# Four hand-set orders instead of one, and other PSUM banks and another order of the expert pairs for the last two batches

## The reference

```
x = x + L0_attn(layernorm(x))   # 16 heads of 8, softmax over 256 keys, relative positions clipped at 20
x = x + L0_ffn(layernorm(x))    # per token: attention of its 16 heads among each other, then 8 experts, softmax gate
x = x + L1_attn(layernorm(x))   # 8 heads of 16, second-order Taylor expansion of exp, linear attention
x = x + L1_ffn(layernorm(x))    # router, top 2 of 8 experts, and one shared expert
# an expert of L1_ffn: silu((x @ w1 + b1) * (x @ w3 + b3)) @ w2 + b2, hidden width 176
```

## Time and profile before

| what | value |
|---|---|
| median of 3 runs | 770.97 us (770.21 to 772.57) |
| the profiled execution's own time | 772.51 us |
| its span (first to last instruction) | 770.7 us |
| PE busy | 659.4 us (86%) |
| DVE busy | 554.9 us (72%) |
| ACT busy | 387.9 us (50%) |
| mean granted clock of PE | 0.955 |

### The profile page before, as it was taken

The page is one execution under the profiler, slowest core; times in us unless marked ns, Lnnn a source line. Parts: engine busy times, 40 slices in busy tenths (PEclk is TensorE's granted clock), DMA queues, the critical chain, the costliest instruction groups (busy, mean ns, idle before and its releaser), DMA issues. The chain is left out here.

```text
span 770.7 us, 16746 instructions
## 1 busy us (share of the span) xinstructions
PE 659.4 (86%) x6432; PEld 520.3 (68%) x6432; DVE 554.9 (72%) x1337; ACT 387.9 (50%) x907; POOL 146.0 (19%) x178
## 2 busy tenths in 40 slices
PE   2688566987999999999999999999998997787886
PEld 1567445765787788778777787678776874565655
DVE  2322578569768986899679977898679867876263
ACT  3365235446556754674556555656565544225240
POOL 2413201330233023300520051104220101011000
PEclk9999787999899999999999999999999999799798
DMA  5502000200110002000200011001100010000000
GB/s 126 217 1 22 15 1 1 26 12 2 14 16 9 1 15 22 9 1 2 27 17 1 2 23 21 1 2 21 16 1 2 8 16 1 0 8 1 0 8 7
DMA packets 75908, 13.43 MB, mean 17 GB/s; under 512 B 69803, under 2 KB 74933, under 8 KB 75701
## 3 DMA queue, kind: packets, MB, share of 16 engines
q1 hardware_dynamic: 73202, 10.78, 7.8%
q0 software_dynamic: 384, 1.05, 0.5%
q10 hardware_dynamic: 2244, 0.55, 0.3%
HBM read 8.95 MB, written 3.16 MB: 16 GB/s over the span
## 5 line engine op out<-in xcount | busy, mean ns | idle before, releaser
L475 ACT ACTIVATE pm<-bank,nmx 128x256 f32<-128x256 f32 x256 | 100.6, 476 | 129.5 <-DVE nmx L760 129.5
L760 DVE TENSOR_REDUCE nmx<-bank 128x2 f32<-128x512 f32 x128 | 82.2, 684 | 48.9 <-PE bank L1083 48.8
L1094 PE MATMUL bank<-w,pm 128*128 128x128 f32 x512 | 83.3, 288 | 22.4 <-ACT pT L483 15.5
L483 ACT ACTIVATE pT<-bank 128x512 f32<-128x512 f32 x128 | 77.0, 602 | 43.7 <-PE bank L1094 42.5
L1073 PE MATMUL bank<-kT,qbd 64*64 64x256 f32 x1024 | 90.1, 415 | 9.4 <-POOL qr L585 9.3
L1112 PE MATMUL bank<-tv,pT 128*128 128x128 f32 (+1 forms) x512 | 81.0, 281 | 7.5 <-ACT pT L483 7.5
L1094 PEld LDWEIGHTS bank<-w,pm 128*128 128x128 f32 x512 | 60.9, 147 | 37.8 <-ACT pm L475 20.8
L970 DVE SCALAR_TENSOR_TENSOR hu<-bank,w,ha 128x256 f32<-128x256 f32 x104 | 49.9, 481 | 48.8 <-ACT ha L540 48.5
L1112 PEld LDWEIGHTS bank<-tv,pT 128*128 128x128 f32 x512 | 68.9, 193 | 16.8 <-issue 8.2
L540 ACT ACTIVATE ha<-bank,w 128x256 f32<-128x256 f32 x104 | 49.8, 479 | 48.9 <-PE bank L1272 48.9
L1271 PE MATMUL bank<-xfT,w 128*128 128x256 f32 x208 | 66.4, 401 | 7.5 <-DVE hu L970 7.4
(11 more groups left out here) (202 smaller groups left out, 1305.8 us busy)
## 6 DMA issues: line engine op xcount, KB each, us to landing
w<-wpack_dram SPq DMA_DIRECT2D x1, 3944.0 KB, 12.2
xin<-x_in_dram SPq DMA_DIRECT2D x8, 128.0 KB, 2.1
d_qdh<-qdh SPq DMA_DIRECT2D x8, 128.0 KB, 2.1
d_rv<-rvs SPq DMA_DIRECT2D x64, 16.0 KB, 2.2
out_dram<-xo POOLq DMA_DIRECT2D x8, 128.0 KB, 2.6
qc<-d_qdh SPq DMA_DIRECT2D x15, 64.0 KB, 3.8
tv<-d_ev SPq DMA_DIRECT2D x1, 736.0 KB, 4.5
w<-wpack_dram SPq DMA_DIRECT2D x1, 513.0 KB, 4.5
```

Of the source, the lines that this page charges most:

```text
L475: a = act.activation(pm[:, s % 2, c, j], b_s[c][:, j * S:(j + 1) * S], exp, bias=nmx[:, i:i + 1])
L483: act.activation(view(pT, (c * RTC + 2 * s) * C * P, [[1, 2 * C * P]]), b_t[:], copy).then_inc(pT_ready[0], 1)
L760: v.tensor_reduce(nmx[:, i:i + 2], b_s[c][:].rearrange("p (j k) -> p j k", j=2), AX_X, ALU.max, negate=True).then_inc(max_ready[0], 1)
L1094: a = nc.tensor.transpose(b_t[:, (j * 2 + kc) * P:(j * 2 + kc + 1) * P], chunk(pm[:, s % 2, c, j], kc), ident)
```

## The change

1. **Places by engine.** TURNS becomes one list for each engine, from ENGINE_AT, which has 141 places for each of PE, ACT, DVE and POOL. MOVED shifts the places of batches 0, 6 and 7 (all engines alike). Pieces, batches and instructions stay the same; only the order on each engine's queue differs.
2. **Chunks in another order, for all batches.** IN_TURN makes chunk 3k and 3k+1 the main parts of experts 2k and 2k+1, and chunk 3k+2 their remainder. Joins 0 to 3 are now the expert pairs and join 4 the shared expert. Join n < 4 waits only for the hid_ready that covers its three chunks; in batches 6 and 7 the order places the joins between or right behind the chunks.
3. **Banks of L1_ffn in batches 6 and 7**: chunks in banks 0 and 3, turn_rw in bank 2, joins in banks 1 and 2 in turn.
4. **Batch 7 only**: experts alternate between banks 6 and 4; Taylor scores rotate over banks 6, 4 and 5.

```diff
+IN_TURN = [x for k in range(NP) for x in (2 * k, 2 * k + 1, NX + k)] + [NE]
...
-TURNS = [(t, piece) for _, _, _, t, piece in sorted([(t * STEP[k] + at, at, k, t, piece) for at, k, piece in PIECES for t in range(B)])]
+def in_turn(at):
+    placed = [(t * PERIOD + at[k] + (MOVED[t][k] if t in MOVED else 0), k, t) for k in range(len(ALL)) for t in range(B)]
+    return [(t, ALL[k]) for _, k, t in sorted(placed)]
+TURNS = {engine: in_turn(at) for engine, at in ENGINE_AT.items()}
...
+        def late_bank(t, name, n):
+            if t < B - 2:
+                return bank[3]
+            return {"route": bank[3], "chunk": bank[3 * (n % 2)], "turn_rw": bank[2], "join": bank[1 + n % 2]}[name]
+        def expert_bank(t, n):
+            return b_rv if t == B - 1 and n % 2 else b_a
+        def taylor_bank(t, h):
+            if t < B - 1:
+                return (b_b, b_a)[h % 2]
+            return (b_a, b_rv, b_o)[h % 3]
...
 # PE, experts
+                    elif t < B - 1:
+                        pe.wait_ge(*raised(acc_e, t, 2 * C * n))
+                    elif n == 1:
+                        pe.wait_ge(*raised(rv_kept, B, 0))
                     else:
-                        pe.wait_ge(*raised(acc_e, t, 2 * C * n))
+                        pe.wait_ge(*raised(acc_e, t, 2 * C * (n - 1)))
...
 # PE, taylor
-                    if n == 2:
-                        pe.wait_ge(*raised(o3t_ready, t, 1))
-                    pe.wait_ge(*raised(sq_ready, t, 2 * n))
+                    if t < B - 1:
+                        if n == 2:
+                            pe.wait_ge(*raised(o3t_ready, t, 1))
+                        pe.wait_ge(*raised(sq_ready, t, 2 * n))
+                    elif n == 0:
+                        pe.wait_ge(*raised(acc_e, t, 2 * NE))
+                        pe.wait_ge(*raised(x1_ready, t, 1))
+                    else:
+                        pe.wait_ge(*raised(sq_ready, t, 2 * n - 1))
...
 # PE, join
-                    if n == 0:
+                    late_free(t, "join", n)
+                    if n == NP:
+                        pe.wait_ge(*raised(rwT_ready, t, 1))
                         pe.wait_ge(*raised(hid_ready, t, HPAIRS))
+                    else:
+                        pe.wait_ge(*raised(hid_ready, t, (3 * n + 2) // 2 + 1))
...
+            def late_free(t, name, n):
+                before = late_before(t, name, n)
+                if before is None:
+                    return
+                was, k = before
+                if was == "route":
+                    pe.wait_ge(*raised(r_steps, t, 2))
+                elif was == "chunk":
+                    pe.wait_ge(*raised(u_ready, t, k + 1))
+                elif was == "turn_rw":
+                    pe.wait_ge(*raised(rwT_ready, t, 1))
+                else:
+                    pe.wait_ge(*raised(eo_acc, t, 2 * C * (k + 1)))
```

More of the change, by code:

```diff
@@ L323, in build, with late_before, turns @@
         block = ctx.enter_context(nc.Block())
[L325 to L335, removed]
+        def late_bank(t, name, n):
+            if t < B - 2:
+                return bank[3]
+            return {"route": bank[3], "chunk": bank[3 * (n % 2)], "turn_rw": bank[2], "join": bank[1 + n % 2]}[name]
+        def late_before(t, name, n):
+            used = [p for p in LATE if p[0] in ("route", "turn_rw", "join") or p[0] == "chunk" and p[1] < NCH]
+            same = [p for p in used[:used.index((name, n))] if late_bank(t, *p) is late_bank(t, name, n)]
+            return same[-1] if same else None
+        def expert_bank(t, n):
[4 more added lines that the diff above has]
+            return (b_a, b_rv, b_o)[h % 3]
+        def turns(engine, piece):
+            for t, (name, n) in TURNS[engine]:
                 piece(t, name, n)
@@ L549, in rest @@
                 elif name == "turn_rw":
-                    evict(t, rwT_ps, 1, rwT_ready, late_bank(t, NCH)[0:NX, 0:S], rwT[:], (eo_ps, t, 0))
+                    evict(t, rwT_ps, 1, rwT_ready, late_bank(t, "turn_rw", 0)[0:NX, 0:S], rwT[:], (eo_ps, t, 0))
             fill_ends()
             act.wait_ge(ones_set[0], 1)
-            turns(piece)
+            turns("ACT", piece)
         @block.gpsimd
@@ L639, in _ @@
             pool.wait_ge(ones_set[0], 1)
-            turns(piece)
+            turns("POOL", piece)
         @block.vector
@@ L1224, in rest @@
                             rows = half * P // 2
-                            a = mm((b_b, b_a)[half][:, kc * S:(kc + 1) * S], chunk(k3[rows:rows + P // 2], kc), q3h[rows:rows + P // 2, n],
+                            a = mm(taylor_bank(t, 2 * n + half)[:, kc * S:(kc + 1) * S], chunk(k3[rows:rows + P // 2], kc), q3h[rows:rows + P // 2, n],
                                    start=True, stop=True, tile_position=(rows, 0))
@@ L1266, in rest @@
                     if n < NCH:
[L1267 to L1272 removed]
+                        late_free(t, "chunk", n)
@@ L1273, in rest @@
+                        bk, q = late_bank(t, "chunk", n), IN_TURN[n]
+                        mm(bk[:, 0:S], wc("W1", q * P, q * P + P), xfT[:], start=True, stop=True)
+                        mm(bk[:, S:2 * S], wc("W3", q * P, q * P + P), xfT[:], start=True, stop=True).then_inc(ab_ps[0], 1)
                 elif name == "turn_rw":
                     pe.wait_ge(*raised(rw_ready, t, 1))
-                    pe.wait_ge(*raised(u_ready, t, NCH + 1 - late_banks(t)))
+                    late_free(t, "turn_rw", 0)
@@ L1276, in rest @@
                     for c in range(C):
-                        a = nc.tensor.transpose(late_bank(t, NCH)[0:NX, c * P:(c + 1) * P], rw[:, c], ident)
+                        a = nc.tensor.transpose(late_bank(t, "turn_rw", 0)[0:NX, c * P:(c + 1) * P], rw[:, c], ident)
                     a.then_inc(rwT_ps[0], 1)
                 elif name == "join":
-                    dst = late_bank(t, n + 1)
-                    if n == 0:
+                    dst = late_bank(t, "join", n)
+                    late_free(t, "join", n)
@@ L1305, in _ @@
             pe.wait_ge(w_in0[0], 16)
-            turns(piece)
+            turns("PE", piece)
 def kernel(**inputs):
```

71 lines of the change are left out of this document (33 added, 38 removed), and 39 rows, old and new, of tables (ENGINE_AT, MOVED).

## The result

| | before | after |
|---|---|---|
| median, run side by side | 771.77 us (770.21 to 775.05, 4 runs) | 739.84 us (737.42 to 742.6, 4 runs) |
| the profiled execution's own time | 772.51 us | 742.6 us |
| its span | 770.7 us | 740.8 us |
| mean granted clock of PE | 0.955 | 0.964 |

What follows compares the result with a forecast made beforehand. PE was taken to bind in the middle and batch 7's chain in the tail. Terms 0.9 + 1.6 + 1.6 + 2.2 + 7.5 + 6.0 = 19.8 us, off 770.97, gave 751.2 us; range 742 to 762.

Steps and rivals of the forecast that it cites:

- from turn3 to route: Batch 7's Taylor scores to route: 7.5 us gained through extra banks and new order, bounds 3 and 9.
- The sign on batch 7's x1: A check on the mechanism: DVE finishes batch 7's x1 within 3 us of 633, against 635.7 before.
- L1_ffn of batch 7: Last stretch: joins start earlier and the 2.56 us wait goes; 6.0 us gained, bounds 3 and 7.
- the head: Batch 0's start: work moves ahead of the relative values' DMA wait and transposes move away; 0.9 us gained.
- The middle: Full batches: the wait for the routing weights' copy is hidden, 0.4 us each, 1.6 us over four.
- The bound of idle time: In the middle only PE's idle time can be won: at most 4.1 us a batch, some 20 in five.
- the wait for the routing weights: PE's wait for their copy in full batches, 0.4 us each, hidden by pieces between turn_rw and join 0.
- the middle gains as well: Rival: half of the 4.1 us idle goes in each of five batches, 10 us, giving 741 to 745; chance 0.12.
- Up to norm3: Batch 7 from x1 to norm3: 1.2 us from DVE's earlier mix sum plus 2.2 in the experts.
- The experts: Batch 7's experts: bank waits and products between them go, norm3 comes earlier; 2.2 us gained, bounds 0 and 3.
- The clock falls: Rival: PE's half-clock stretches in the tail stay or move, costing 4.8 or 5 us, giving 756 to 761; chance 0.13.
- The order holds up the tail: Rival: late PE joins stop DVE, half of the tail's 7.5 and 6.0 us goes, 758 to 762; chance 0.10.

Runs made afterwards that it cites:

- e3: The changed kernel with the old order on all engines from batch 0's project_out to batch 7's; 748.05 us, ratio to before 0.972.
- e7: The changed kernel with the old order on all engines, except ACT's new order up to batch 0's project_out; 762.93 us, ratio to before 0.988.
- e4: The changed kernel with the old order on all engines behind batch 7's project_out, new banks and waits kept; 748.31 us, ratio to before 0.972.
- e6: e4 with batch 7's old banks and their old waits for experts and Taylor scores; 752.53 us, ratio to before 0.975.
- e5: e4 with every join of a pair in batches 5, 6 and 7 also waiting for the last hid_ready; 753.96 us, ratio to before 0.974.
- e12: The changed kernel with only PE and ACT in the old order from batch 0's project_out to batch 7's; 755.02 us, ratio to before 0.982.
- e11: The changed kernel with the old order, except PE's and ACT's new order up to batch 0's project_out; 753.96 us, ratio to before 0.980.
- e1: The changed kernel with all four engines in the old order up to batch 0's project_out; 744.88 us, ratio to before 0.968.
- e2: The changed kernel with only ACT in the old order up to batch 0's project_out; 745.21 us, ratio to before 0.967.
- e8: The changed kernel with batch 7's chunks rotating over four banks (0, 3, 6, 7); 739.71 us, ratio to before 0.958.
- e9: The changed kernel with batch 7's chunks over four banks and its tanh in two buffers; 738.52 us, ratio to before 0.959.
- e10: The changed kernel with two tanh buffers in batch 7, chunks still in banks 0 and 3; 739.32 us, ratio to before 0.961.

## Why the prediction was wrong

**The direction and the tail were right.** 7.5 us from turn3 to route were forecast and 7.5 measured, with the signs that it named: 28 us, clock 1.00, the shared expert in 2.5 us (708.39 to 710.86). The sign on batch 7's x1 failed: it was to be within 3 us of 633 and is at 624.4. For L1_ffn of batch 7 6.0 were forecast, 5.7 came. The 2.56 us wait is gone, and from the last main chunk on the joins follow one another.

**The step that failed is the head.** The sum took 0.9 us for it, 5.8 came (by one profile each, and the head varies by some 2 us, see the last section). The 0.9 was worked out from the one wait at 77.4 us and the transposes at 84.34, the end of the head. For what lies before, the text looked at the page's clock and at no timeline. There batch 0 is alone with its scores, ACT and PE hand each other pm and pT, and PE waits for pT 6.8 us in seven places. The diff has a MOVED row for batch 0 alone, which said that this stretch would change.

**The middle was too small.** Of 5.5 us, 2.0 were in the sum. The bound of idle time was right (20 us), and so was the guess that the full batches give little: 0.5 us each by e3, 0.3 between before and after, where 0.4 were forecast for the wait for the routing weights. That wait is indeed gone from PE's list in the full batches (1.3 us in three before), but waits for ACT's squares came in (3.8 us in five). But "middle" was read from a full batch and applied to all. The first gap (73.4 us before, 70.9 after) and the last (76.5 and 75.5) aren't as full as the others (PE works 53.7 of 73.5 us in the first, 70.9 of 76.5 in the last), and by e3 they are worth 2.7 and 1.9 of the 7.4. The rival "the middle gains as well" (10 us, 741 to 745) named the direction, but with 2 us in each full batch, which did not come.

**Up to norm3** 3.4 us were forecast (1.2 and 2.2), 5.5 came. The experts gave 2.3 (8.6 to 6.3), so that term held. The stretch ahead of them gave 3.2 instead of 1.2. The sum had no clock in it for this stretch, and the mean clock there rose from 0.84 to 0.93. Why it rose is not shown: the joins of batch 5 no longer wait for their last chunk, which the text left out, but e7 has that too and keeps the 0.84.

**The causes were credited wrongly inside a right number.** In the tail the text ascribed the clock and the waits to order and banks together, and I expected e4, without the order, to lose most of it. It lost 4.8 of 18.6 us. The joins' early start and the banks carry more than the order.

**The rivals.** "The clock falls" did not come where it was priced, from turn3 on: the clock is at 1.00 from 650 us on. Between batch 7's x1 and there it still fell, to 0.50 at 648 us. The Trainium skill (TensorE: Matmul & The Clock Gate, "A second HAM failure mode: psum-queue depth-cycling") ties a swinging clock to cycling through banks with short idle times between groups. The runs agree in that: with the old banks (e6) the waits of 0.46 and 1.19 us and the half clock come back together. That more banks need not help was my own inference in the prediction; the section says nothing of the number of banks. It did not hold here: with a third bank the 1.19 us wait fell to 0.62, and the clock from turn3 to route is 0.95 in e4 instead of 0.85 in e6. Banks alone don't secure it either: e5 has them and is at 0.86. "The order holds up the tail" did not happen with these four lists, and e12 shows that it was no idle fear: in the middle, two new lists with two old ones cost 14.6 us against four new ones, and 7.2 against four old ones.

**The sum by the runs.** From before to e7, banks and expert pairs: 1.2%, 9 us. From e7 to e11, PE's and ACT's order in the head: 0.9%, 7 us. From e11 to the change, all other order: 1.9%, 15 us.

## What to carry to other kernels

Cut a pipelined kernel at the same marks in every batch and read every stretch between, the first batch's above all: a full batch tells nothing of those where the pipeline fills and empties, and this order by hand gave most there. Lists for engines are one object: change all that hand work to each other or none, since half a change gained 0 in the head and lost 7 us in the middle. Where a loop of two engines sets the rhythm, look for the second loop of the same length behind it before you open the first: alone four banks gave 1.7 us, a second tile nothing, both 3.0 (of 26.0 in that stretch). And read the granted clock of a stretch beside its length: two executions of one order differ by it, and a wait that is gone can be worth more through the clock than by its own length.

## What the runs showed that was not expected

The same order of instructions does not always take the same time, and where it differs is the lightly loaded head and the stretch ahead of batch 7's experts (48.5 to 50.0 us in after, e1, e2, e8, e9 and e10). The ten executions with the new head on PE and ACT have batch 0's x1 between 78.7 (e12) and 81.2 us (e6). From turn3 to route, executions of the same order and banks give 28.08 or 28.09 us each time. The clock differs in the head too. The first slices of e4, which has the head of the changed kernel:

```profile
PEclk9999679999999999999999999999999999999999
```

Its second slice is a 9, where the changed kernel's is a 7; by five-us windows from 20 to 30 us the changed kernel and e3 are at 0.50 and 0.6, e6 and e11 at 1.00, with the same PE order up to there. Yet e3 has its x1 at 78.8 and e6 at 81.2, so the clock of these ten us does not order the results, and what does stays open. A stretch from turn3 to route can tell 0.1 us by one profile, the head no less than 2.

The head's gain does not add up. With the new order in the middle, taking the head's order away costs 4.1 us at batch 0's x1 and 1.8 at batch 7's (626.21 against 624.38); with the old middle, e7 to e11, it is 6.4 and 4.5. So the changed middle may make up for a late start in part. It is not shown: the seven executions with the change's order up to there have batch 7's x1 between 621.3 (e10) and 625.1 us (e6), e1 is only 1.1 above that, and in the medians e1 is 5.0 us slower.
